# GpSimd's order in the first step of an item: the addition for q's second chunk ahead of the low part of the normalised tokens

## What is computed

```python
for i in range(DEPTH):                       # DEPTH = 6
    x = attn_layer(shift_tokens(x), Wqkv[i], q_scale[i], k_scale[i], Wo[i]) + x
    x = ffn_layer(shift_tokens(x), ln_g[i], ln_b[i], W1[i], b1[i], W2[i], b2[i]) + x

def attn_layer(x, Wqkv, qs, ksc, Wo):        # 16 heads of 64, windows of 32 tokens
    q, k, v = jnp.split(x @ Wqkv, 3, -1)
    q, k = l2norm(q) * qs, l2norm(k) * ksc
    q, k = rotary(q), rotary(k)              # q * cos + rotate_half(q) * sin
    return local_attention(q, k, v) @ Wo

def ffn_layer(x, g, bln, W1, b1, W2, b2):
    xn = (x - mean) / sqrt(var + 1e-5) * g + bln
    a, gate = jnp.split(xn @ W1 + b1, 2, -1)
    return a * gelu(gate) @ W2 + b2
```

## Time and profile before

| | us |
|---|---|
| median of 3 runs | 1683.49 |
| lowest, highest | 1682.31, 1683.5 |
| the profiled execution, its own time | 1678.35 |
| its span, first to last instruction | 1676.6 |
| PE busy | 1568.2 (94%) |
| DVE busy | 1447.6 (86%) |
| ACT busy | 1114.9 (66%) |
| POOL busy | 1068.4 (64%) |

### The profile page before, as it was taken

One profiled execution on the slowest core, in us unless ns is written; L12 is line 12 of the kernel. 1 busy time (PEld: TensorE's weight loads), 2 busy tenths in 40 slices (PEclk: granted clock), 3 DMA queues, 4 the chain that ended last, 5 costly groups with the idle time before them and its releaser, 6 DMA issues.

```text
span 1676.6 us, 77736 instructions
## 1 busy us (share of the span) xinstructions
PE 1568.2 (94%) x33168; PEld 1271.4 (76%) x33168; DVE 1447.6 (86%) x3173; ACT 1114.9 (66%) x2014; POOL 1068.4 (64%) x1040
## 2 busy tenths in 40 slices
PE   4469999999999999999999999999999999999987
PEld 2247888778878878888778788788887878887874
DVE  8969989889889888889989889888889888898862
ACT  4336677667677667677667766766776766776663
POOL 3646767676666666667576577585676575675640
PEclk7679999999999999999999999999999999999999
DMA  2011111211111211111211111211111111111110
GB/s 88 32 51 45 41 38 40 77 35 41 34 50 38 60 44 40 42 51 29 63 38 53 43 37 42 63 38 53 30 51 41 50 51 47 32 44 41 38 47 14
DMA packets 41086, 75.09 MB, mean 45 GB/s; under 512 B 9472, under 2 KB 22568, under 8 KB 40744
## 3 DMA queue, kind: packets, MB, share of 16 engines
q1 hardware_dynamic: 40744, 70.12, 14.4%
HBM read 20.08 MB, written 2.10 MB: 13 GB/s over the span
## 4 chain that ended last, share of the span: by engine, by line
PE 68%; issue 8%; POOL 8%; DVE 6%; ACT 5%; ACTq 0%; POOLq 0%; DVEq 0%
PE bank L1372 8%; PE bank L1340 7%; PE bank L1423 7%; PE bank L1497 7%; PE wide L1465 7%; PE bank L1342 6%; PE bank L1341 6%; PE bank L1482 4%; PE bank L1577 4%; PE bank L1442 3%; POOL qk L864 3%; POOL qk L872 2%; PE bank L1411 2%; PE bank L1549 2%; PE bank L1553 1%
## 5 line engine op out<-in xcount | busy, mean ns | idle before, releaser
L872 POOL TENSOR_TENSOR qk<-qk,rnorm 128x512 f32<-128x512 f32 x384 | 401.2, 1045 | 344.4 <-DVE rnorm L1025 344.4
L864 POOL TENSOR_TENSOR qk<-qk,qk_sin 128x512 f32<-128x512 f32 x384 | 491.8, 1281 | 146.3 <-DVE qk_sin L986 146.3
L1188 ACT ACTIVATE squares<-bank 128x512 f32<-128x512 f32 x384 | 229.5, 598 | 153.5 <-DVE qk_sin L986 153.3
L996 DVE TENSOR_REDUCE norm<-squares 128x8 f32<-128x512 f32 x384 | 258.5, 678 | 30.5 <-ACT squares L1188 28.3
L1340 PE MATMUL bank<-w_hi,xs_hi 128*128 128x512 f32 x576 | 263.5, 457 | 11.8 <-ACT squares L1188 6.6
L979 DVE TENSOR_TENSOR qk<-bank,tables 128x512 f32<-128x512 f32 x384 | 261.7, 682 | 8.8 <-PE bank L1342 8.6
L986 DVE TENSOR_TENSOR qk_sin<-bank,tables 128x512 f32<-128x512 f32 x384 | 261.4, 681 | 0.6 <-POOL qk L864 0.6
L1372 PE MATMUL bank<-ident,qk 128*128 128x128 f32 x1536 | 225.3, 278 | 6.1 <-POOL qk L872 5.3
L1342 PE MATMUL bank<-w_hi,xs_lo 128*128 128x512 f32 x576 | 228.9, 397 | 0.0
L1341 PE MATMUL bank<-w_lo,xs_hi 128*128 128x512 f32 x576 | 227.9, 396 | 0.4 <-issue 0.4
L1372 PEld LDWEIGHTS bank<-ident,qk 128*128 128x128 f32 x1536 | 180.8, 141 | 44.4 <-POOL qk L872 7.0
(11 more groups left out here) (181 smaller groups left out, 2724.9 us busy)
## 6 DMA issues: line engine op xcount, KB each, us to landing
v<-v SPq DMA_DIRECT2D x96, 390.0 KB, 3.5
v<-v SPq DMA_DIRECT2D x72, 130.0 KB, 3.6
w_raw<-in_L_ffn_Wqkv SPq DMA_DIRECT2D x36, 256.0 KB, 3.2
w_o_s<-in_L_ffn_Wo SPq DMA_DIRECT2D x6, 512.0 KB, 3.9
w_raw<-in_L_ffn_W SPq DMA_DIRECT2D x6, 341.0 KB, 3.4
mix_x_nat<-in_L_attn_x SPq DMA_DIRECT2D x4, 256.0 KB, 3.4
w_raw<-x_res_scratch SPq DMA_DIRECT2D x4, 256.0 KB, 3.4
out<-w_raw SPq DMA_DIRECT2D x4, 256.0 KB, 3.2
```

What stands on the lines that cost most here:

```text
L864: pool.tensor_tensor(qk[:, g % 2, c, :], qk[:, g % 2, c, :], qk_sin[:, (QK_CHUNKS * g + c) % SINES, :], ALU.add).then_inc(added[c], 1)
L872: pool.tensor_tensor(view, view, rnorm[:, g % 2, c * HPC:(c + 1) * HPC].unsqueeze(2) .to_broadcast([P, HPC, DH]), ALU.mult).then_inc(norme ...
L996: dve.tensor_reduce(norm2[:, c * HPC:(c + 1) * HPC], squares[:, c % 2, :].rearrange("p (h d) -> p h d", d=DH), AX.X, ALU.add).then_inc(sum ...
```

## The change

Two calls in GpSimd's loop trade places: `add(step, 1)` now stands ahead of the `if t == 0: split_xn(item - 2)`. In steps with t of 1, 2 or 3 `split_xn` isn't called, so the order there is the same as before. In the first steps of items 2 to 23, 22 in number, both are called, and the two instructions stand the other way round. In items 0 and 1 there is no `split_xn`; in the two first steps behind item 23 there is no `add`. No instruction is added or taken away, no wait is changed, and the lists of the other engines are as they were.

```diff
                 if opening:
                     split_weights(layer, V1)
                 normalise(step - 1, 2)
+                add(step, 1)
                 if t == 0:
                     split_xn(item - 2)
-                add(step, 1)
                 if ending:
                     split_weights(layer + 1, K0)
                 if t == NBLK - 1:
```

## The result

| | before | changed |
|---|---|---|
| median of 6 runs, us | 1682.12 | 1690.89 |
| lowest, highest | 1680.09, 1683.5 | 1687.97, 1695.75 |
| ratio, 95% interval | | 1.0048 (1.0034 to 1.0062) |
| profiled execution, span | 1676.6 | 1694.0 |

The changed kernel is slower by 0.48%, which is 8.1 us (5.7 to 10.4) on 1682.12. The prediction said +4.45 us, 1687.9, with a range up to 1690.2; the median lies 0.7 us above that range. The direction was right, and the cost is 1.8 times the forecast.

The account below looks back on a forecast made before the run. TensorE, busy 94%, was taken as the bound, waiting on GpSimd in five opening steps. Earlier add 0, ordinary steps 17 x 0, opening steps 5 x 0.89 = 4.45 us on 1683.49 gave 1687.9 us, range 1684.5 to 1690.2.

Parts of the forecast that it names:

- Where the time is set: TensorE waits for GpSimd's xn_lo in five opening steps, where later is slower; 17 ordinary first steps have room, cost 0.
- the earlier `add`: GpSimd's add of chunk 1 starts earlier by one xn_lo; worth nothing, since an earlier end frees nobody.
- The sum of an opening step: In each opening step xn_lo and L1553 come 1.25 us later, TensorE reaches turn_qk of chunk 1 0.89 us later.
- The term of the 0.36 us won back at `turn_qk`: Opening steps: normalise of chunk 1 isn't moved, so 0.36 us of L1553's later start is room before turn_qk.
- the first five of the six signs: L1553's wait about 10.3 us; L872 waits about 5; 2.6 us L1553 to L1372; TensorE releases gelu; GpSimd L857 distance unchanged.
- The sixth: Time from one opening step to the next grows by 0.89 us; 1.25 would mean B, 0.3 would mean C.
- case E, the clock: TensorE standing 2.13 us per opening step brings 10 us at clock 0.50 each: +25 us, 1713; chance 0.03.
- B: Opening steps lose the 0.36 us again at expand of j = 1 because hidden is late: 6.25 us, 1689.7; chance 0.11.
- C: A later issue gap behind each opening step takes up to 0.62 us of its delay: 1.4 us, 1684.9; chance 0.14.
- D: Not slower: earlier add brings GpSimd's later work forward where ScalarE's bias is late; 1681.7, or 1678.2; chance 0.08.

Follow-up runs that it names:

- the first comparison: The two calls trade places in the 17 ordinary first steps only, against the kernel before: 1.0012 (1.0002 to 1.0021), +2.0 us.
- the second: The same kernel, order changed in the 17 ordinary first steps only, measured once more against the kernel before: 0.9998 (0.9986 to 1.001).
- the three profiles with the move: Changed kernel (1.0048), changed kernel again (1.0047), and the first kernel with the calls traded in the five opening steps only (1.0045, +7.6 us).
- filled waits: Changed kernel plus 8 idle matmuls in each of five waits, 8 fewer mask pieces in the same steps: 1.0018 (1.0009 to 1.0027), +3.0 us against before.

## Why the prediction was right or wrong

*Where the time is set* was right. TensorE waits for `xn_lo` five times, in the opening steps, and nowhere else; the ordinary steps, 1.0012 on the first comparison and 0.9998 on the second, cost nothing that can be measured; and nothing shows a gain from the earlier `add`.

*The sum of an opening step* was right: +0.89 was forecast, 0.85 to 0.90 was measured in all nine opening steps of the three profiles with the move in which the clock held, and in the five with filled waits. The term of the 0.36 us won back at `turn_qk` held, too: 2.58 us from L1553 to L1372, with no wait. So did the first five of the six signs: 10.4 us in 5 waits against 10.3 forecast, 5 waits for L872 of 4.0 us, the 2.58 us where the clock held, GpSimd's L857 in item 12 3.45 us behind the start of the L872 ahead of the traded pair (3.48 before), and a gelu let go by TensorE, as ScalarE's timeline in item 12 shows (an idle 0.96 us behind its table load):

```profile
862.91 1.28 ACT L1261 ACT_TABLE_LOAD   x1
865.15 0.69 ACT L1261 ACTIVATE xsq_gated<-bank,vecs 128x512 f32<-128x512 f32 x1 [0.96 <-PE bank L1553]
```

The sixth, growth by 0.89 us from one opening step to the next, came true in three of the five opening steps of each profile; in the other two it was 2.2 to 2.3 us, which none of its readings foresaw.

*The step that failed is case E, the clock.* It was among the rivals with the right mechanism and place, but with a chance of 0.03, with a price per fall taken from a stretch of 10 us, and as something that happens in every opening step or in none; the sum itself had no term for it. The runs showed 1.37 us for each fall, in two of five opening steps in all three profiles: 5 x 0.88 + 2 x 1.37 = 7.1 us against a measured 8.1 (5.7 to 10.4). The argument against it was that TensorE was busy for only 2.87 us of the 5 between 1645 and 1650 us and kept the upper level. That was the mistake. Those 2.13 us were in several pieces and in one execution that happened to show no fall. The second profile of the same kernel showed two there: one at the wait of 1.51 us before L1497, and one at the end of the very same stretch, which begins at 1647.70 in it, with 137 matmuls for 138 and the same waits of 0.73 and 1.05 us:

```profile
1647.70:1652.70 5.00, 3.22 (x137) 2.50 (x135) 2.04 (x5) 1.07 (x2) 0.00 (x0) 0.86 0.02 5
```

The clock is 0.86 in the mean, where the earlier trace rows has 1.00. One stretch of one profile can show that a pause may pass, not that it will. The waits had the number that mattered: between 200 and 1500 us no wait of TensorE was longer than 0.9 us in the first profile, and the change made five of them 2.1.

*The rivals.* B, the whole 1.25 us, comes nearer the total (6.25 us) for the wrong reason; the opening steps without a fall exclude it. C, the delay taken up by gaps called issue, has nothing for it: with the move those gaps were 20.0, 13.3 and 12.5 us in three profiles, without it 14.1 and 15.9, and in all three comparisons with the move the time grew by at least as much as the opening steps did, 7.6 to 8.1 us against 7.1 or 7.2. Only the +3.0 us (1.5 to 4.5) of the kernel with filled waits would leave room for a part of it. The Trainium skill, "Runtime: NRT & Kernel Launch", section "Instruction fetch mechanics", whose rule would make C, calls the cost of crossing a block of instructions "mostly hidden". If the waits called issue are that cost, which no run here shows by itself, the trace disagrees: in the kernel with 40 more matmuls they went from 21.7 to 46.2 us. D needed ScalarE to be late, and in none of the 22 steps with both calls was it.

What stays open: which opening steps lose the clock (12 and 16, 12 and 20, 8 and 20), why it was two each time, and the 1 us between the 7.1 us of the opening steps and the 8.1 measured, which is within the interval.

## What to carry to other kernels

When an edit lengthens a wait of TensorE, compare the new length with the longest ones that the profile has in steady running, gaps called issue included: if nothing that long is there, the granted clock behind it is a term of the sum, with a share of the waits and a price of its own, and not a remote case. A wait that looks costly may be only the first of two on one chain: taking away the one for `xn_lo` gained nothing until the work that ends the chain, `normalise` of chunk 1, was moved ahead, and then 4.2 us. In an experiment that adds instructions to a long list, hold their number, or the result is that of another layout.

## What was not expected of the hardware

- The fall of the clock in an opening step grew more frequent with the pause, but wasn't certain: it fell behind pauses of about 2.1 us in 6 of 15, of 2.7 us in 5 of 5, of 1.4 us in 0 of 5, of 0.9 us in 0 of 20. Each fall in the three profiles with the move cost 1.37 us, with a pass of 512 columns at 0.43 us instead of 0.23. Elsewhere a pause of 1.5 us was enough in some executions.
- Eight idle bf16 matmuls in the wait, 1.90 us, kept the upper level in 10 of 10. With the number of instructions held, the opening steps grew by 4.4 us instead of 7.1, and the kernel's time by 3.0 instead of about 8.
- Forty more matmuls on TensorE, in five places, cost 33 us, most of it by waits called issue that lay elsewhere and later. With as many others taken out in the same steps, that cost was gone. Why the place of an instruction in the list matters so much is not shown.
- The same kernel's last part took 4.1 us more in one execution than in another, with the clock falling in the one, first at a wait of 1.51 us, and not in the other. A difference between two single profiles has to be split up by place before it is read.
